# A graph network kernel: the node features and the weights are loaded from ScalarE's DMA queue, and a matrix is zeroed in rows of 5000 bytes

## The chip, the cores and the metric

The kernel runs on one core of a Trainium2 chip. The time is device time in microseconds of one execution. The program has five engines: TensorE (PE), VectorE (DVE), ScalarE (ACT), GpSimd (POOL) and SyncE (SP). SP, ACT and POOL can issue DMAs. The profile names their queues q1 (SP), q10 (ACT) and q0 (POOL). All of them move their data on the same 16 DMA engines.

## The reference

Four graph layers run one after the other on 3125 nodes with 256 features and 50,000 edges, whose destinations are sorted. Each layer normalises the features, and gathers those of the neighbours:

```
h = relu(layernorm(x));  x = x + L0(h)   # sum over edges, two products with batch norm
h = relu(layernorm(x));  x = x + L1(h)   # two weighted graph convolutions, W1, W2, Wl
h = relu(layernorm(x));  x = x + L2(h)   # one convolution, scaled by the degrees
h = relu(layernorm(x));  x = x + L3(h)   # two attention layers, 4 heads and 1
```

`_L0_gnn_ref` and `_L2_gnn_ref` use how often an edge occurs, `_L1_gnn_ref` the sum of its `edge_weight`.

## The kernel before

The kernel turns the edge list into dense matrices first. `pairs` in HBM holds for each destination and each source two numbers: the sum of the edges' weights and their count. It has 25 blocks (`NB`) of 128 destinations with 3125 sources, which is 25,000 bytes for a destination, 3.2 MB for a block and 80 MB in all. The stages that matter here are:

1. SP loads `dst`, `src`, `edge_weight` and the features `X`, then writes zeros over all 25 blocks. At most `ZQ` = 4 of these transfers are in flight: from the fifth on, SP waits for the transfer four places back, and raises `zero_ok`. Behind the last one SP issues 28 small loads (the weights and per-feature values), which all raise `w_in`.
2. DVE makes the keys of the edges (`e1`, `e2`, `key_c`), PE transposes them, ACT copies the transposed weights (`wgt`, L1000) and DVE the transposed keys (L1219). Both raise `edges_laid`, and nothing of what follows starts before both have.
3. 50 rounds (`NSC`) of 1000 edges each: PE and DVE find edges that occur twice (`same`, L1249) and sum them up (`merged`, L1271). In round 3 DVE waits for `X`, in round 30 for `w_in` (L1317).
4. POOL scatters each finished round into `pairs`, with 8 indirect DMAs that add (L555). Round t needs `merged` of t, the zeroed blocks up to `zero_ok`, and that all scatters of the round before have landed.
5. When all 50 rounds are merged, SP loads `pairs` back in 40 pieces, in rows of 5000 bytes (`pair_load`, L398). They form eight groups of 4, 4, 4, 4, 4, 2, 2 and 1 blocks with five pieces each, and a group waits until POOL's rounds that touch it are done. PE multiplies them with the features (L672) and transposes them (L692), and ACT stores the transposes (L1025, L1028) for the layers that follow.

The order of the work on each queue is the order in the code. The lines of ACT's part begin with the copy of stage 2, and there is no DMA ahead of it.

Of the kernel before, what the change touches and what calls it, by code (L numbers as in the profile page):

```python
# [16 lines left out]
Q = 125  # L17
NB = N // Q
D = 256
KT = D // 128  # L20
# [8 lines left out]
EA = 4  # L29
ECC = EC // EA  # L30
ZQ = 4
ZR = 25
KB = SC // 4
TRASH = ROWS * N
HALF = [(0, 13), (13, 12)]
# [58 lines left out]
def gnn_stack(nc, x, src, dst, edge_weight, eps0, W01, b01, g01, be01, W02, b02, g02, be02,  # L94
              W11, b11, W12, b12, Wl1, bl1, root_idx, W2, b2, W31, as31, ad31, b31, gnw, gnb, gnms,
              W32, as32, ad32, b32, out):
    with ExitStack() as ctx:
        sems = {}

        def S(name):  # L100
            if name not in sems:
                sems[name] = ctx.enter_context(nc.semaphore(name))
            return sems[name]

        def sb(name, shape, dt=F32):
            return ctx.enter_context(nc.sbuf_tensor(name, shape, dt))
# [11 lines left out]
        X = sb("X", [128, NB, D])  # L118
# [38 lines left out]
        w01, w02, w11 = [wA[:, k * KT * D:(k + 1) * KT * D].rearrange("p (k n) -> p k n", k=KT) for k in range(3)]  # L157
        w12 = wA[:, 3 * KT * D:5 * KT * D].rearrange("p (k n) -> p k n", k=2 * KT)
        wB = sb("wB", [128, 4 * KT * D])
        wl1 = wB[:, 0:2 * KT * D].rearrange("p (k n) -> p k n", k=2 * KT)  # L160
        w2, w2T = [wB[:, k * KT * D:(k + 1) * KT * D].rearrange("p (k n) -> p k n", k=KT) for k in (2, 3)]
# [7 lines left out]
        w32 = sb("w32", [128, CT, D + 2])  # L169
        va = sb("va", [128, KT, 2 * HEADS])  # L170
        cols = sb("cols", [128, 6, KT])
        colw = sb("colw", [128, 4, CT])
        bcs = sb("bcs", [128, 5, D])
        ident = sb("ident", [128, 128])
        ones = sb("ones", [128, 128])
        small = sb("small", [128, 40])
# [26 lines left out]
        idx_i = sb("idx_i", [128, 1], I32)  # L203
# [36 lines left out]
        att2 = [B[:, 2 * WIDE:2 * WIDE + D], B[:, 2 * WIDE + D:2 * WIDE + 2 * D]]  # L240
# [103 lines left out]
        colb = sb("colb", [128, 2 * KT])  # L344

        @block.sync
        def _(sp):
# [2 lines left out]
            sp.dma_start(wgt_c, edge_weight.rearrange("(c k) -> c k", k=CW)).then_inc(S("wgt_in"), 16)  # L350


            sp.dma_start(X[0:Q, :, :], x.rearrange("(j p) f -> p j f", p=Q)).then_inc(S("x_in"), 16)
            sp.wait_ge(S("zero_made"), 1)
            flat = pairs[0:TRASH, :].rearrange("(i p r c) t -> i p r (c t)", p=128, r=ZR, c=N // ZR)
            zero = R[:, 0:2 * N // ZR].unsqueeze(1).to_broadcast([128, ZR, 2 * N // ZR])
            sp.dma_start(pairs[TRASH:TRASH + SC * 128, :].rearrange("(p c) t -> p (c t)", p=128),
                         R[:, 0:2 * SC]).then_inc(S("zero_tail"), 16)
            for i in range(NB + ZQ):
# [2 lines left out]
                    sp.sem_inc(S("zero_ok"), 1)  # L362
                if i < NB:
                    sp.dma_start(flat[i], zero).then_inc(S(f"zeroed{i % ZQ}"), 16)
            w_in = S("w_in")
            nw = 0
            for t, w in ((w01, W01), (w02, W02), (w11, W11), (w12, W12), (wl1, Wl1), (w2, W2)):
                sp.dma_start(t[:, :, :], w.rearrange("(k p) n -> p k n", p=128)).then_inc(w_in, 16)
                nw += 1
            sp.dma_start(w32[:, :, 0:D], W32.rearrange("(k p) n -> p k n", p=128)).then_inc(w_in, 16)  # L370
            for k, a in enumerate((as32, ad32)):
                sp.dma_start(att2[k], a.rearrange("h c -> (h c)").partition_broadcast(128)).then_inc(w_in, 16)
            for k, v in enumerate((b11, b12, bl1, b2, b32)):
                sp.dma_start(bcs[:, k, :], v.partition_broadcast(128)).then_inc(w_in, 16)
            sp.dma_start(idx_i[:, 0:1], root_idx[0:1].partition_broadcast(128)).then_inc(w_in, 16)
            sp.dma_start(small[:, 0:1], eps0.partition_broadcast(128)).then_inc(w_in, 16)
            with nc.allow_non_contiguous_dma(reason="a few hundred per-feature values"):
                for k, v in enumerate((b01, g01, be01, b02, g02, be02)):
                    sp.dma_start(cols[:, k, :], v.rearrange("(k p) -> p k", p=128)).then_inc(w_in, 16)
                for k, v in enumerate((b12, b11)):  # L380
                    sp.dma_start(colb[:, k * KT:(k + 1) * KT], v.rearrange("(k p) -> p k", p=128)).then_inc(w_in, 16)
                for k, v in enumerate((b31, gnw, gnb, gnms)):
                    sp.dma_start(colw[:, k, :], v.rearrange("(k p) -> p k", p=128)).then_inc(w_in, 16)

            def pair_load(i):
                g, part = PUNITS[i]
                j0, nb = PG[g]
                if part == 0:  # L390
                    windows = sp.value_load(rneed[0:1, g:g + 1], min_val=1, max_val=NSC)
                    sp.wait_ge(S("rounds_done"), windows)
                    sp.sem_inc(S("pairs_begun"), 1)
                if i >= 2:
                    sp.wait_ge(S("l0_pe"), 4 * (i - 1))
                    sp.wait_ge(S("tr_pe"), PB * (i - 1))
                    sp.wait_ge(S("deg_done"), i - 1)
                sp.dma_start(PR[i % 2][:, 0:nb, :, :],  # L398
                             pair_rows[j0:j0 + nb, :, part * PW:(part + 1) * PW, :].rearrange("m p c t -> p m c t"))\
                    .then_inc(S(f"prow{i % 2}"), 16)  # L400
# [15 lines left out]
            for q in range(4 * NB):  # L416
                k, j = divmod(q, NB)
                c0, w = HALF[k % 2][0] * Q, COLS[k % 2]
# [3 lines left out]
            for q in range(4 * NB, 6 * NB):  # L422
                k, j = divmod(q, NB)
                c0, w = HALF[k % 2][0] * Q, COLS[k % 2]
                n = q - 4 * NB
# [45 lines left out]
            for q in range(STEPS * NB):  # L471
                k, j = divmod(q, NB)
# [37 lines left out]
            for q in range(STEPS * NB + LCR, (STEPS + 2) * NB):  # L510
                k, j = divmod(q, NB)
# [482 lines left out]
        @block.scalar  # L994
        def _(act):
            a = nc.scalar.activation


            act.wait_ge(S("edgeT"), 1)
# [31 lines left out]
            for i, (g, part) in enumerate(PUNITS):  # L1031
# [5 lines left out]
                for b in range(PB):  # L1037
                    n = PB * i + b
# [57 lines left out]
            for q in range(4 * NB, 6 * NB):  # L1096
                n = q - 4 * NB
                k, j = divmod(q, NB)
                w = COLS[k % 2]
# [81 lines left out]
        def _(dve):  # L1181
# [3 lines left out]

            v_.memset(R[:, 0:2 * N // ZR], 0.0).then_inc(S("zero_made"), 1)
            link.mark(v_.memset(val, 0.0))
# [645 lines left out]
```

## Time and profile before

| | |
|---|---|
| median of 3 timed runs | 4287.06 us (4277.83 to 4291.34) |
| the profiled execution | 4239.87 us |
| its span | 4238.1 us |
| busy: PE, DVE, ACT, POOL | 3434.9, 2683.2, 833.4, 650.4 us |
| moved by DMA | 523.88 MB, of it 159.74 MB written to HBM |

The span is cut into 40 slices of 106 us on the page, with a digit for the busy tenths of each engine. "Idle before, releaser" is the time in which an engine stood still ahead of an instruction, and what ended it. A queue that is called SPq or ACTq is the sequencer of that engine, which issues the DMAs; the time of such a row is how long the issue kept the engine.

### The profile page before, as it was taken

To read this page: it belongs to the slowest core of one execution; us is meant where nothing else is said; L and a number is where in the kernel's file an instruction comes from. 1 tells how busy PE (TensorE), PEld (TensorE's weight loads), DVE (VectorE), ACT (ScalarE), POOL (GpSimd) and SP (SyncE) were. 2 spreads that over 40 slices of the span, in tenths; PEclk is the share of its full clock that TensorE was granted. 3 is DMA by queue.
4 is the path that set the end of the run, shared out by engine and by line. 5 is a ranking of instruction groups with operands and counts; after the bars stand their busy time and mean duration, and the time that the engine had idled before them with its cause. 6 is when DMAs were issued, how large, how long until landed. Compare 5 with 4: busy or idle time off the path is not lost. (4 is left out here: it accounts for less than half of the span.)

```text
span 4238.1 us, 32521 instructions
## 1 busy us (share of the span) xinstructions
PE 3434.9 (81%) x12169; PEld 2015.7 (48%) x12169; DVE 2683.2 (63%) x3582; ACT 833.4 (20%) x1091; POOL 650.4 (15%) x462
## 2 busy tenths in 40 slices
PE   6830889956889999979952788888888899975898
PEld 6830867745545555444441343444344344454444
DVE  9931933312330111143449999999999999956997
ACT  0010023312420000122300222222222222232222
POOL 2555765666100000000000000000000000011000
PEclk6555589978999999989965999999999999987999
DMA  9999179967624334412135212222222223256222
GB/s 203 226 227 178 2 226 315 290 186 184 170 87 138 124 126 137 147 40 72 55 108 177 59 55 60 86 73 66 73 66 70 63 90 90 71 180 218 74 67 67
DMA packets 311726, 523.88 MB, mean 124 GB/s; under 512 B 91521, under 2 KB 232727, under 8 KB 310039
## 3 DMA queue, kind: packets, MB, share of 16 engines
q1 hardware_dynamic: 197489, 441.36, 36.1%
q0 software_dynamic: 61600, 20.44, 4.6%
q10 hardware_dynamic: 52480, 60.01, 4.4%
q8 instruction: 96, 1.57, 0.2%
q14 instruction: 61, 0.50, 0.0%
HBM read 361.99 MB, written 159.74 MB: 123 GB/s over the span
## 5 line engine op out<-in xcount | busy, mean ns | idle before, releaser
L935 PE MATMUL ps<-R,B 125*128 125x500 f32 x2800 | 1118.3, 552 | 91.7 <-DVE R L1710 87.0
L935 PEld LDWEIGHTS ps<-R,B 125*128 125x128 f32 x2800 | 513.3, 194 | 668.1 <-issue 543.0
L555 POOL DMA_INDIRECT pairs<-w x400 | 620.6, 1552 | 448.6 <-issue 257.1
L788 PE MATMUL ps<-R,H 125*128 125x500 f32 (+1 forms) x1400 | 554.0, 552 | 35.0 <-DVE R L1496 21.7
L1124 ACT ACTIVATE R<-R,asc 125x1625 f32<-125x1625 f32 (+1 forms) x200 | 320.1, 1601 | 1189.6 <-DVE R L1697 1189.5
L563 POOL DMA_DIRECT2D B<-ct_d x50 | 27.1, 546 | 2792.6 <-PE ps L935 2656.1
L1710 DVE SCALAR_TENSOR_TENSOR R<-R 125x1625 f32<-125x1625 f32 (+1 forms) x250 | 444.7, 1779 | 0.0
L788 PEld LDWEIGHTS ps<-R,H 125*128 125x128 f32 x1400 | 258.5, 195 | 316.4 <-issue 313.7
L645 PE MATMUL ps<-Fb,R 125*125 125x4 bf16 x1800 | 234.5, 248 | 202.7 <-DVE R L1249 194.7
L1697 DVE SCALAR_TENSOR_TENSOR R<-H,asc 125x1625 f32<-125x1625 f32 (+1 forms) x200 | 367.7, 1839 | 34.1 <-PE ps L935 28.0
L672 PE MATMUL ps<-R,H 125*128 125x375 f32 (+1 forms) x1000 | 305.1, 453 | 86.8 <-DMA R<-pairs 86.8
L1585 DVE SCALAR_TENSOR_TENSOR Fb<-R,asc,Fb 125x1625 f32<-125x1625 uint16 (+1 forms) x192 | 353.7, 1842 | 5.2 <-DVE ag L1610 0.2
L645 PEld LDWEIGHTS ps<-Fb,R 125*125 125x125 bf16 x1800 | 224.5, 219 | 218.6 <-issue 162.0
L935 PE MATMUL ps<-R,H 125*128 125x500 f32 (+1 forms) x700 | 276.6, 552 | 21.2 <-DVE R L1710 19.5
L1346 DVE TENSOR_TENSOR Fb<-Fb,ps 128x250 f32<-128x250 f32 (+1 forms) x140 | 67.3, 481 | 352.1 <-PE ps L672 292.6
L788 PE MATMUL ps<-R,B 125*128 125x500 f32 (+1 forms) x700 | 266.8, 538 | 1.6 <-ACT R L1081 0.9
L672 PEld LDWEIGHTS ps<-R,H 125*128 125x128 f32 x1000 | 188.1, 196 | 163.2 <-DMA R<-pairs 76.7
L1249 DVE SCALAR_TENSOR_TENSOR R<-ps,Fb,R 125x500 bf16<-125x500 f32 (+3 forms) x400 | 205.4, 536 | 2.3 <-PE ps L634 2.3
L1677 DVE TENSOR_TENSOR wB<-wB,R 125x1500 f32<-125x1500 f32 x120 | 205.6, 1713 | 0.2
L935 PEld LDWEIGHTS ps<-R,H 125*128 125x128 f32 x700 | 127.1, 194 | 164.6 <-issue 132.5
L692 PE MATMUL ps<-ident,R 125*125 125x125 f32 x1250 | 171.0, 285 | 32.0 <-ACT PT L1041 24.5
L788 PEld LDWEIGHTS ps<-R,B 125*128 125x128 f32 x700 | 126.9, 190 | 140.6 <-issue 139.4
(262 smaller groups left out, 3005.1 us busy)
## 6 DMA issues: line engine op xcount, KB each, us to landing
pairs<-R SPq DMA_DIRECT2D x25, 3125.0 KB, 38.3
R<-ct_d SPq DMA_DIRECT2D x175, 406.2 KB, 3.2
R<-ct_d SPq DMA_DIRECT2D x175, 375.0 KB, 3.1
R<-pairs SPq DMA_DIRECT2D x25, 2500.0 KB, 10.1
R<-wt_d SPq DMA_DIRECT2D x50, 812.5 KB, 4.4
R<-wt_d SPq DMA_DIRECT2D x50, 750.0 KB, 4.2
wt_d<-R ACTq DMA_DIRECT2D x13, 1250.0 KB, 7.6
wt_d<-B ACTq DMA_DIRECT2D x12, 1250.0 KB, 7.6
```

The lines of the kernel that those rows point to most:

```text
L555: pool.indirect_dma_start(pairs, bass.IndirectOffsetOnAxis(ap=key_u[:, c:c + 1], axis=0), val[:, c, :], None, compute_op=ALU.add).then_inc ...
L645: last = mm(ps[0:Q, 4 + t % 2, c * 4:(c + 1) * 4], TW[c0][:, c * Q:(c + 1) * Q], vals[:, t * SC + c0, :], start=c0 == 0 and c == 0, stop=c ...
L672: last = mm(ps[:, n % 4, 0:w], H[0:Q, j0 + m, k * 128:(k + 1) * 128], PR[i % 2][0:Q, m, o:o + w, 0], start=m == 0, stop=m == nb - 1 and no ...
L692: last = tr(ps[0:Q, 4 + 2 * (n % 2) + t, m * Q:(m + 1) * Q], PR[i % 2][0:Q, m, b * Q:(b + 1) * Q, t], ident[0:Q, 0:Q])
L788: last = mm(ps[:, bank, at:at + w], rows[0:Q, j, f * 128:(f + 1) * 128], TL[q % TS][0:Q, o:o + w], start=j == 0 and at == 0, stop=j == NB ...
L935: last = mm(ps[:, bank, at:at + w], rows[0:Q, j, f * 128:(f + 1) * 128], TT[q % TR][0:Q, o:o + w], start=j == 0 and at == 0, stop=j == NB ...
L1124: a(t, t, ACT.Exp, bias=s2).then_inc(S("l3_exp"), 1)
L1249: last = stt(TW[c][:, b * CW + lo:(b + 1) * CW], ps[0:Q, (t % 2) * 2 + b, lo:CW], k, mask, ALU.is_equal, ALU.mult, accum_out=later[0:Q, t ...
L1585: stt(dst, t, score, dst, ALU.min, ALU.max).then_inc(S(name), 1)
L1677: tt(d, d, t, ALU.add).then_inc(S("l3_den"), 1)
L1697: stt(TT[q % TR][0:Q, 0:w], u[0:Q, 0:w], s8, u[0:Q, w:2 * w], ALU.add, ALU.max).then_inc(S("l3_a"), 1)
L1710: stt(t, t, 1.0, lc, ALU.min, ALU.mult).then_inc(S("l3_t"), 1)
```

## The change

`ZR`, the number of rows into which a destination's 25,000 bytes are cut, goes from 25 to 5, so that a block is zeroed in 640 rows of 5000 bytes and not in 3200 rows of 1000. The zeros that are read come from `R[:, 0:1250]`, so DVE clears 1250 columns there and not 250. The load of `X` and the 28 loads of `w_in` leave SP's program. They stand at the start of ACT's, ahead of its first wait.

```
-ZR = 25
+ZR = 5
...
-            sp.dma_start(X[0:Q, :, :], x.rearrange("(j p) f -> p j f", p=Q)).then_inc(S("x_in"), 16)
             sp.wait_ge(S("zero_made"), 1)
             flat = pairs[0:TRASH, :].rearrange("(i p r c) t -> i p r (c t)", p=128, r=ZR, c=N // ZR)
             zero = R[:, 0:2 * N // ZR].unsqueeze(1).to_broadcast([128, ZR, 2 * N // ZR])
...
                 if i < NB:
                     sp.dma_start(flat[i], zero).then_inc(S(f"zeroed{i % ZQ}"), 16)
-            w_in = S("w_in")
-            nw = 0
-            for t, w in ((w01, W01), (w02, W02), (w11, W11), (w12, W12), (wl1, Wl1), (w2, W2)):
-                sp.dma_start(t[:, :, :], w.rearrange("(k p) n -> p k n", p=128)).then_inc(w_in, 16)
-                nw += 1
-            sp.dma_start(w32[:, :, 0:D], W32.rearrange("(k p) n -> p k n", p=128)).then_inc(w_in, 16)
...
         @block.scalar
         def _(act):
             a = nc.scalar.activation
+            act.dma_start(X[0:Q, :, :], x.rearrange("(j p) f -> p j f", p=Q)).then_inc(S("x_in"), 16)
+            w_in = S("w_in")
+            for t, w in ((w01, W01), (w02, W02), (w11, W11), (w12, W12), (wl1, Wl1), (w2, W2)):
+                act.dma_start(t[:, :, :], w.rearrange("(k p) n -> p k n", p=128)).then_inc(w_in, 16)
+            act.dma_start(w32[:, :, 0:D], W32.rearrange("(k p) n -> p k n", p=128)).then_inc(w_in, 16)
...
             act.wait_ge(S("edgeT"), 1)
```

The start of ACT's program before, where the first two rows are the table load and the copy that `edges_laid` waits for, and the third is the next table load:

```order
L1000 ACT_TABLE_LOAD
L1000 ACTIVATE Fb<-ps 125x4x100
L1008 ACT_TABLE_LOAD
L1008 ACTIVATE lns<-lns 125x25
L1011 ACTIVATE H<-X,lns 125x256 x25
```

The same place now (`wA` and `wB` hold the weights, `w` is `w32`):

```order
L974 DMA X<-in_x 125x25x256
L977 DMA wA<-in_L_gnn_W 128x2x256 x3
L977 DMA wA<-in_L_gnn_W 128x4x256
L977 DMA wB<-in_L_gnn_Wl 128x4x256
L977 DMA wB<-in_L_gnn_W 128x2x256
L978 DMA w<-in_L_gnn_W 128x8x256
L980 DMA B<-in_L_gnn_att_src 128x256
L991 DMA colw<-in_L_gnn_gn_ms 128x8x1
L995 ACT_TABLE_LOAD
L995 ACTIVATE Fb<-ps 125x4x100
```

The load of `X` and 28 more DMAs (of which some rows are left out here) now stand ahead of the copy.

The start of SP's program before, where `Fb` takes the edge list and the L357 row is a small tail of `pairs`:

```order
L348 DMA Fb<-in_dst 100x500
L349 DMA Fb<-in_src 100x500
L350 DMA Fb<-in_edge_weight 100x500
L353 DMA X<-in_x 125x25x256
L357 DMA pairs<-R 128x16
L364 DMA pairs<-R 3200x1x250 x25
L368 DMA wA<-in_L_gnn_W 128x2x256 x3
```

And now:

```order
L348 DMA Fb<-in_dst 100x500
L349 DMA Fb<-in_src 100x500
L350 DMA Fb<-in_edge_weight 100x500
L356 DMA pairs<-R 128x16
L363 DMA pairs<-R 640x1x1250 x25
L368 TENSOR_LOAD rneed
```

The zeroing moved up behind the three small loads, with 640 rows in a transfer, and the register load of the first `pair_load` follows it at once.

## Rows read from the trace of the kernel before

**Rows 1.** The page: busy tenths of the 40 slices, and the DMA engines' share.

```profile
DVE  9931933312330111143449999999999999956997
...
POOL 2555765666100000000000000000000000011000
...
DMA  9999179967624334412135212222222223256222
```

**Rows 2.** Timeline of POOL: start, duration, instruction, idle before.

```profile
65.69 1.79 POOL L555 DMA_INDIRECT pairs<-w  x1 [62.17 <-SPq L362]
...
387.75 1.55 POOL L555 DMA_INDIRECT pairs<-w  x1 [5.65 <-DMA pairs<-w]
...
426.91 1.55 POOL L555 DMA_INDIRECT pairs<-w  x1 [2.35 <-DMA pairs<-w]
...
443.64 1.55 POOL L555 DMA_INDIRECT pairs<-w  x1 [2.20 <-issue]
...
460.32 1.55 POOL L555 DMA_INDIRECT pairs<-w  x1 [2.15 <-issue]
...
1058.18 1.55 POOL L555 DMA_INDIRECT pairs<-w  x1 [4.53 <-issue]
```

**Rows 3.** Timeline of PE in the stage of the loads, and its end.

```profile
897.11 7.75 PE L672 MATMUL ps<-R,H 125*128 125x375 f32 x16 [49.73 <-DMA R<-pairs]
...
1044.26 4.92 PE L672 MATMUL ps<-R,H 125*128 125x375 f32 x8 [24.74 <-DMA R<-pairs]
...
1123.27 0.61 PE L672 MATMUL ps<-R,H 125*128 125x250 f32 x2
```

**Rows 4.** Waits up to 900 us: engine and line, waited for, us, times, longest.

```profile
DVE small L1317 <- DMA colw<-in_L_gnn_gn_ms: 157.4, 1, 157.4
...
SPq L391 <- DVE w L1271: 137.0, 1, 137.0
```

**Rows 5.** Timeline: DVE's clearing, the copy, the first duplicate search, the first merged round.

```profile
0.94 0.27 DVE L1186 MEMSET R<- 128x250 f32 x1 [0.94 <-PEq L1823]
...
18.25 0.87 ACT L1000 ACTIVATE Fb<-ps 125x400 f32<-125x400 f32 x1 [16.15 <-PE ps L623]
...
26.59 0.74 DVE L1249 SCALAR_TENSOR_TENSOR R<-ps,Fb,R 125x500 bf16<-125x500 f32 x1 [2.26 <-PE ps L634]
...
38.65 0.17 DVE L1271 TENSOR_TENSOR w<-keyf,trash 125x8 uint32<-125x8 f32 x1
```

**Rows 6.** Timeline of SP's queue: the issues, and how long each kept SP.

```profile
2.02 0.31 SPq L353 DMA_DIRECT2D X<-in_x  x1
2.37 25.06 SPq L357 DMA_DIRECT2D pairs<-R  x1
27.48 339.32 SPq L364 DMA_DIRECT2D pairs<-R  x25
388.52 1.94 SPq L368 DMA_DIRECT2D wA<-in_L_gnn_W  x4
...
409.52 0.58 SPq L383 DMA_DIRECT2D colw<-in_L_gnn_gn_ms  x1
548.10 340.79 SPq L398 DMA_DIRECT2D R<-pairs  x22
```

**Rows 7.** DMA engines' busy tenths from 0 to 60 us, 1.5 us a digit.

```profile
DMA  0463333333333333333999999999999999999999
```

**Rows 8.** Windows: stretch, busy by engine, granted clock, DMA share, GB/s.

```profile
28.50:33.00 4.50, 2.95 (x30) 2.57 (x29) 4.50 (x21) 0.00 (x0) 0.00 (x0) 0.82 1.01 335
35.00:64.00 29.00, 24.71 (x173) 23.26 (x172) 28.66 (x125) 0.00 (x0) 0.00 (x0) 0.50 1.12 238
...
554.00:558.00 4.00, 0.61 (x1) 0.50 (x2) 0.65 (x4) 0.00 (x0) 3.39 (x3) 0.50 1.11 381
```

**Rows 9.** DMA queues from 985 to 989 us: packets, MB, share.

```profile
q1 hardware_dynamic: 225, 1.05, 70.2%
...
q10 hardware_dynamic: 59, 0.05, 4.3%
```

**Rows 10.** The same from 990 to 992 us, where ACT's queue runs alone.

```profile
q10 hardware_dynamic: 614, 0.61, 92.8%
```

**Rows 11.** The same from 388 to 412 us, the 28 loads of `w_in`.

```profile
q1 hardware_dynamic: 10816, 4.09, 72.3%
```

**Rows 12.** The same from 945 to 949 us, beside scatters issued at 945.19 and 947.05.

```profile
q1 hardware_dynamic: 289, 1.45, 96.2%
```

**Rows 13.** One line of the kernel, L364: ns min, median, max of an issue.

```profile
L364 SPq DMA_DIRECT2D pairs<-R x25: 627/14252/15327, 27.5 to 352.6; - x25
```

More of the change, by code:

```diff
@@ L364, in _ @@
                     sp.dma_start(flat[i], zero).then_inc(S(f"zeroed{i % ZQ}"), 16)
-            w_in = S("w_in")
-            nw = 0
-            for t, w in ((w01, W01), (w02, W02), (w11, W11), (w12, W12), (wl1, Wl1), (w2, W2)):
-                sp.dma_start(t[:, :, :], w.rearrange("(k p) n -> p k n", p=128)).then_inc(w_in, 16)
-                nw += 1
-            sp.dma_start(w32[:, :, 0:D], W32.rearrange("(k p) n -> p k n", p=128)).then_inc(w_in, 16)
[L371 to L383, printed above, removed]
             def pair_load(i):
@@ L996, in _ @@
             a = nc.scalar.activation
+            act.dma_start(X[0:Q, :, :], x.rearrange("(j p) f -> p j f", p=Q)).then_inc(S("x_in"), 16)
[3 more added lines that the diff above has]
+            act.dma_start(w32[:, :, 0:D], W32.rearrange("(k p) n -> p k n", p=128)).then_inc(w_in, 16)
+            for k, row in enumerate((as32, ad32)):
+                act.dma_start(att2[k], row.rearrange("h c -> (h c)").partition_broadcast(128)).then_inc(w_in, 16)
+            for k, v in enumerate((b11, b12, bl1, b2, b32)):
+                act.dma_start(bcs[:, k, :], v.partition_broadcast(128)).then_inc(w_in, 16)
+            act.dma_start(idx_i[:, 0:1], root_idx[0:1].partition_broadcast(128)).then_inc(w_in, 16)
+            act.dma_start(small[:, 0:1], eps0.partition_broadcast(128)).then_inc(w_in, 16)
+            with nc.allow_non_contiguous_dma(reason="a few hundred per-feature values"):
+                for k, v in enumerate((b01, g01, be01, b02, g02, be02)):
+                    act.dma_start(cols[:, k, :], v.rearrange("(k p) -> p k", p=128)).then_inc(w_in, 16)
+                for k, v in enumerate((b12, b11)):
+                    act.dma_start(colb[:, k * KT:(k + 1) * KT], v.rearrange("(k p) -> p k", p=128)).then_inc(w_in, 16)
+                for k, v in enumerate((b31, gnw, gnb, gnms)):
+                    act.dma_start(colw[:, k, :], v.rearrange("(k p) -> p k", p=128)).then_inc(w_in, 16)
             act.wait_ge(S("edgeT"), 1)
```

## The prediction

> **What bounds the kernel now.** The page comes first, for where engines stand still. In slices 3 to 4 DVE falls to 3 and 1 tenths while the DMA engines are at 9, and POOL is busy at a middle level up to slice 10 [rows 1]. So the question is which of them sets when the first layer can start. The waits say that DVE stands 157.4 us for the last load of `w_in`, since those loads are issued behind all the zeroing; SP can therefore start loading `pairs` only at 548.10, after waiting 137.0 us for DVE [rows 4, 6]. That looks like 157 us to be won. The timelines of POOL and PE say otherwise. POOL's 50 rounds run without a pause from 65.69 to 1058.18 [rows 2], and PE waits for loaded pieces at 897.11 (49.73 us) and at 1044.26 (24.74 us), when the groups' rounds weren't done [rows 3]. The stage ends at 1123.9, 65.7 us after POOL's last round starts. **POOL's last round is the bound**; DVE's stop only eats slack, at least until POOL's end moves forward by the 50 us that PE waits at 897.
>
> POOL's rounds have three speeds, which I read from the starts of their first scatters. Beside the zeroing, 14 rounds from 65.69 to 387.75: 23.0 us each. With quiet DMA engines, 443.64 to 460.32: 16.7 us. From 426.91 to 1058.18 it is 33 rounds in 631.3 us, 80 us more than 33 x 16.7 = 551; that is what the loads and stores of the product stage cost POOL [rows 2]. A later last round follows from a start S and the zeroing's end Z: rounds at the slow speed until Z, then 16.7 each, and 80 on top.
>
> **Zeroing in 5000-byte rows.** 25 blocks of 3.2 MB are 80 MB. In rows of 1000 bytes they go at 238 GB/s, after a burst of 335 in the first 4.5 us; the loads of `pairs`, whose rows have 5000 bytes, go at 381, though they read HBM [rows 8]. So the rate lies between 238 (HBM takes no more, whatever the rows) and 381 (the engines' own pace), which is 336 to 210 us. I take 285, the middle between the sustained rate and the burst: the burst shows that short rows aren't all that limits, the drop behind it that writing may be. That is 281 us, and from a start at about 4 us Z = 285. The bounds for Z are 245 (335 GB/s; beside `X` it won't be more) and 345. Clearing 1250 columns in place of 250 is five times 0.27 us at most [rows 5], some 1 us at the start; I neglect it.
>
> **The loads on ACT's queue.** This decides. An issue is short only when the queue can take it. SP issued `X` in 0.31 us, but its next DMA, a tiny one, kept SP for 25.06 us [rows 6]: until `X` had nearly drained. The zeroing's issues of 3200 rows kept SP 14.25 us each in the median [rows 13]. I read that as: an issue is held until the one before it has been turned into rows that the engines have mostly consumed. ACT must pay the same: `X`, 28 issues behind it, and only then the copy at L995, which ran at 18.25 before [rows 5]. Behind the copy stand the key rows, the duplicate search (8.3 us later) and the first merged round (20.6 us later), and so POOL's first scatter.
>
> How long is ACT held? With nothing beside it: 25 us for `X` and 22 us for the rest (388.52 to about 410) [rows 6], so 48. But the zeroing is beside it. `X` uses only some of the engines: the digits are 3 while it runs, about 5 of 16 [rows 7], which is 3125 / 5 = 625 rows on each, 26 us / 625 = 42 ns a row. The best row on sharing is 985 to 989 us: ACT's last 1000-byte rows beside SP's 5000-byte rows come at 59 in 4 us, 15 a us, while alone ACT's queue does 614 in 2 us, 307 a us [rows 9, 10]. Some engines will have run out of ACT's rows there, so 15 is too low a bound; but it fits an engine that takes rows from its queues by turns, one long for one short, and no split by bytes. By turns, each row of `X` waits for a row of zeros of 210 ns (5000 bytes at 381/16 GB/s) to 336 ns (at 238/16): 625 x 0.25 to 0.38 = 158 to 236 us. Of the 1000 rows of zeros that each engine has (25 x 40) 375 are then left, beside 10816 / 16 = 676 packets of the 28 loads [rows 11]. So the zeroing ends first, and the remaining 300 packets go at their own pace, 300/676 of 22 us = 10 us. **ACT is free at about Z + 10 = 295 us**, 277 later than now. If the zeros and ACT's rows were generated by one unit in order of issue, ACT's 28 issues would each wait behind one of the 25 blocks, and the answer is the same.
>
> [...]
>
> **The sum.** S = 295 + 20.6 = 316, when the zeroing is over, so all rounds have the quiet speed: last round at 316 + 49 x 16.7 + 80 = 1214, against 1058. That is +156 us; what follows the last round keeps its 66 us, and all later layers their times. The stage of the loads starts at about 295 + 8 + 364 = 667 (DVE's search took 548 - 27 - 157 = 364 without its stop), when POOL is at round 21, so PE goes on waiting for POOL and the removed 157 us stop is worth nothing. The faster rounds beside no zeroing are worth 14 x 6.3 = 88 us, and are in the sum. 4240 + 156 = 4396 for the profiled execution; the timed runs' median stands 47 us above that, so 4287 + 156 = **4443 us, say 4440**. Bounds from Z: 245 gives +116, 345 gives +216; its own range is 4400 to 4505.
>
> **Rivals.** (1) ACT is held for `X` only, and the small loads slip through, or turns favour ACT's short rows: free at about 190, S = 211, three rounds beside the zeroing at 25 us: 285 + 46 x 16.7 + 80 = 1133, +75, 4360. (2) The queues share by bytes, or the short rows go ahead: ACT free at 48, S = 69, before the zeroing hurts. With (285 - 69)/23 = 9.4 rounds by Z the last starts at 285 + 39.6 x 16.7 + 80 = 1026: -32 us, **4255, faster**. With Z = 220 it is -50, 4237. For it speaks that the 15 a us may come from engines that had run out of ACT's rows; against it, that an engine with half its time for ACT's rows would have finished 59 of them in well under 4 us [rows 9, 10]. It decides at ACT free by 93 us (S = 113, last round 1059). There is a cost in it: a scatter waits behind 5000-byte rows. From 945 to 949 only SP's queue moved packets, although two scatters had been issued [rows 12]; at 30 us a round the gain shrinks to nothing (285 + 41.8 x 16.7 + 80 = 1063), which is (3), no change. (4) Zeroing at 238 GB/s or less, with the full hold: +216 or more.
>
> **Chances and range.** Full hold 0.45, more than 4505 another 0.05, held for `X` alone 0.20: slower 0.70. Rival 2 is 0.23, no change 0.07. About 0.3% (13 us) is what a measurement can tell. From 4250 to 4520 the range leaves out most of rival 2's better half and the top of rival 4.
>
> **What the profile after would show.** Right: ACTq's second row holds for well over 100 us; the ACT copy at 250 to 355; DVE and PE near 0 in slices 2 and 3; POOL's first scatter 20 us behind the copy and rounds of 16.7; zeroing over at 245 to 345; POOL's last round at about 1214; no wait at DVE's `w_in` line. Wrong: the copy before 93 us, or rounds near 30 us, or POOL's end earlier than 1058. The rate of zeroing is the weakest size, the sharing of engines the weakest step.

## The result and the profile after

| | before | after |
|---|---|---|
| timed runs, one chip | 4282.44 us (4 runs, 4273.53 to 4291.34) | 4355.07 us (4 runs, 4353.93 to 4357.18) |
| span of the profiled execution | 4238.1 us | 4354.0 us |

The ratio is 1.017, with an interval of 1.0146 to 1.0194: 73 us slower in the timed runs, 116 us in the two profiles. The forecast was 156 us slower, 4440 us in the timed runs.

The page after, with the same three rows as [rows 1]:

```profile
DVE  1079973212241111224347999999999999957897
...
POOL 0047775666500000000000000000000000001000
...
DMA  9922239968833343431125312221222223247222
```

The slices are 109 us now. DVE and POOL do next to nothing in the first two, where the DMA engines are busiest. Before, POOL was at 2 and 5 tenths there.

The timeline of ACT, with the issues on its queue. The first row is the load of `X`, the second the first of the 28 behind it, the third the last of them, and then comes the copy that all waits for:

```profile
0.82 0.57 ACTq L974 DMA_DIRECT2D X<-in_x  x1
1.42 115.88 ACTq L977 DMA_DIRECT2D wA<-in_L_gnn_W  x1
...
238.59 3.37 ACTq L991 DMA_DIRECT2D colw<-in_L_gnn_gn_ms  x1
241.99 1.28 ACT L995 ACT_TABLE_LOAD   x1 [241.99 <-issue]
243.29 0.87 ACT L995 ACTIVATE Fb<-ps 125x400 f32<-125x400 f32 x1
```

ACT is held for 242 us, and copies at 243.3 where it copied at 18.3 [rows 5]. The table load, which was made while the engine waited (at 0.82 us in the kernel before), now stands behind the issues too and adds 1.3.

The timeline of POOL:

```profile
265.68 1.79 POOL L532 DMA_INDIRECT pairs<-w  x1 [262.16 <-issue]
282.58 1.55 POOL L532 DMA_INDIRECT pairs<-w  x1 [2.15 <-DMA pairs<-w]
299.38 1.55 POOL L532 DMA_INDIRECT pairs<-w  x1 [2.26 <-DMA pairs<-w]
...
1167.39 1.55 POOL L532 DMA_INDIRECT pairs<-w  x1 [5.70 <-issue]
```

The first scatter is 200 us later than before, the rounds then have the quiet speed of 16.7 to 16.9 us up to the stage of the loads, and the last round starts 109 us later (1167.4 against 1058.2, [rows 2]). The faster rounds gave 91 of the 200 us back. PE still waits for POOL's rounds:

```profile
1000.29 7.49 PE L649 MATMUL ps<-R,H 125*128 125x375 f32 x16 [66.52 <-DMA R<-pairs]
...
1152.40 5.37 PE L649 MATMUL ps<-R,H 125*128 125x375 f32 x8 [26.06 <-DMA R<-pairs]
```

These answer to [rows 3], where it was 49.73 and 24.74 us. The 157.4 us for which DVE stood for `w_in` [rows 4] are gone from the waits, and they brought nothing.

The windows of the zeroing (8 to 110 and 110 to 220 us), columns as in [rows 8], and the DMA digits from 220 to 246 us, 0.65 us a digit:

```profile
8.00:110.00 102.00, 2.49 (x10) 1.87 (x10) 9.70 (x17) 0.00 (x0) 0.00 (x0) 1.00 0.99 394
110.00:220.00 110.00, 0.00 (x0) 0.00 (x0) 0.00 (x0) 0.00 (x0) 0.00 (x0) 1.00 1.01 377
```

```profile
DMA  9999999999565333333333333333348221080000
```

The DMA engines move 394 and 377 GB/s in all. The zeros' share of it, on SP's queue, is 371 and 335 (37.87 and 36.83 MB); from 4 to 227 us it is 78.75 MB, or 353 GB/s, above the 335 that I took as the upper bound. At 227 us the digit falls to 3 (SP's queue takes 30.8% of the 16 engines from 229 to 238 us, about 5), and stays there until about 240. I take these for the five that carried `X` and so have zeros still to write; the profile doesn't name them, but with `X` cut over all engines (`after_xsplit`, below) there is no such stretch: the digits fall from 9 to 0 between 222 and 226 us. ACT is free when they are done.

### The profile page after: what moved, and what is told of

It reads as the page before. It is cut to its first block and busy times, and to the rows that moved or that the text cites. A ratio compares the mean times of both kernels' runs of the same rounds, so it can differ in the third digit from the quotient of the medians.

```text
span 4354.0 us, 32521 instructions
## 1 busy us (share of the span) xinstructions
PE 3449.3 (79%) x12169; PEld 2023.6 (46%) x12169; DVE 2684.8 (62%) x3582; ACT 833.4 (19%) x1091; POOL 650.2 (15%) x462
## 5 line engine op out<-in xcount | busy, mean ns | idle before, releaser
L912 PEld LDWEIGHTS ps<-R,B 125*128 125x128 f32 x2800 | 515.9, 195 | 671.5 <-issue 546.8
L611 PE MATMUL ps<-ident,Fb 125*125 125x125 f32 x400 | 100.8, 433 | 230.2 <-DVE Fb L1230 230.2
```

Source lines behind the costliest of these rows:

```text
L912: last = mm(ps[:, bank, at:at + w], rows[0:Q, j, f * 128:(f + 1) * 128], TT[q % TR][0:Q, o:o + w], start=j == 0 and at == 0, stop=j == NB ...
```

## The experiments

All were timed against the kernel before on their own chip. There the kernel before took 4242 to 4243 us, not 4282. "Last round" is the start of POOL's last round of scatters.

**The kernel before again.** No edit.

> The kernel before, unchanged, so that a second profile of it stands beside timed runs of the same chip. Its profiled execution was 4240 us, its timed runs 4274 to 4291. If the gap is a matter of the chip or the day (theory chip), profile and timed runs of this one agree within 5 us, and their common time shows whether 4240 or 4285 is the rule. If the profiled execution is always shorter than the timed ones (theory profiling), the gap of 40 us comes again. In the trace I look at the rounds of POOL beside the zeroing (23.0 us each before) and at the start of its last round (1058 before).

Measured: 4244.0 us in 10 runs, its profile's span 4245.5, the kernel before 4242.7 in 18 runs; ratio 0.9998 (0.9986 to 1.001). Profile and timed runs agree. So a profiled execution isn't shorter by nature, and 4282 us is particular to the first comparison (its chip or its hour; which of them isn't shown). The last round starts at 1058.77.

**Only the rows.** From the kernel before:

```
-ZR = 25
+ZR = 5
```

> Only ZR = 5; all loads stay on SP, so ACT copies at 18 us. Zeroing from 27 us at 400 GB/s, over at about 230, the loads of w_in done by 255 and no stop of DVE. Theory queue depth: a scatter waits behind a number of rows, so five times as long rows make POOL's rounds beside the zeroing 30 us or more; 5.5 of them, last round at 1037, time 20 us under before. Theory bytes in flight: rounds stay at 23 us, 7 of them, last round at 1008, 50 us under before. If the zeroing in short rows had cost nothing, the time would be that of before.

Measured: 4179.5 us, ratio 0.9843 (0.9818 to 0.9867), 63 us faster. The timeline of POOL:

```profile
42.01 1.79 POOL L555 DMA_INDIRECT pairs<-w  x1 [38.49 <-SPq L362]
64.93 1.55 POOL L555 DMA_INDIRECT pairs<-w  x1 [8.16 <-DMA pairs<-w]
...
227.63 1.55 POOL L555 DMA_INDIRECT pairs<-w  x1 [7.69 <-DMA pairs<-w]
...
996.80 1.55 POOL L555 DMA_INDIRECT pairs<-w  x1 [4.51 <-issue]
```

Eight rounds from 42.01 to 227.63 are 23.2 us each, where 1000-byte rows had 23.0: rows five times as long don't make the scatters beside them slower. POOL also starts 24 us sooner (42.01 against 65.69), as the first block is zeroed sooner; I had not counted that. The last round is at 996.8, where "bytes in flight" had 1008 and "queue depth" 1037.

**The loads on ACT's queue beside short rows.** From the changed kernel:

```
-ZR = 5
+ZR = 25
```

> The change with ZR = 25: loads on ACT's queue, rows of 1000 bytes. Theory turns (each DMA engine takes one row of each queue in turn): a row of X waits for a row of 60 to 70 ns and not of 200, so X takes 65 to 75 us in place of 127, the rest about as long, ACT copies at 130 to 150 us; POOL starts at 150 to 170, 8 to 9 rounds of 23 us beside the zeroing that lasts to 345 to 360, last round at 1100 to 1115, 40 to 60 us over before. Theory bytes (the queues share by bytes): X takes 52 us with any row length, the copy is at 80 to 100, with 5000-byte rows as with these, and the last round comes by 1075.

Measured: 4269.1 us, ratio 1.0066 (1.0045 to 1.0087), 26 us slower. The timeline of ACT:

```profile
1.42 53.34 ACTq L977 DMA_DIRECT2D wA<-in_L_gnn_W  x1
...
108.84 0.87 ACT L995 ACTIVATE Fb<-ps 125x400 f32<-125x400 f32 x1
```

The issue behind `X` holds ACT for 53 us and not for 116, so the length of the other queue's rows matters; but the hold, the copy (109) and the last round (1085.5) were all sooner than "turns" had them, and 53 is also what sharing by bytes gives here. This run alone is not clear between them; the next is.

**And beside rows of 25000 bytes.** The same with

```
-ZR = 5
+ZR = 1
```

> The change with ZR = 1: zeroing in rows of 25000 bytes, 200 on each DMA engine. Theory turns, one row of each queue: the 625 rows of X on its five engines outlast the 200 rows of zeros, so X is done only after the zeroing (215 to 230 us), the issue behind X holds ACT for 220 to 240 us in place of 116, the rest goes alone in 22, ACT copies at 245 to 270, last round at 1170 to 1195, time 5 to 25 us over the changed kernel's. Theory bytes: the hold behind X stays at about 116 us, and the time at the changed kernel's or under it.

Measured: 4335.0 us, ratio 1.0222 (1.0205 to 1.0239), the same as the changed kernel's on that chip. The timeline of ACT, and the queues from 60 to 120 us (packets, MB, share), first for this kernel and then for the changed one:

```profile
1.42 210.71 ACTq L977 DMA_DIRECT2D wA<-in_L_gnn_W  x1
...
238.57 0.87 ACT L995 ACTIVATE Fb<-ps 125x400 f32<-125x400 f32 x1
```

```profile
q1 hardware_dynamic: 1142, 25.48, 99.0%
q10 hardware_dynamic: 345, 0.35, 1.7%
```

```profile
q1 hardware_dynamic: 4377, 21.38, 88.3%
q10 hardware_dynamic: 1302, 1.33, 6.3%
```

SP's packets lie on 16 engines (99.0%), those of `X` on 5: from 5 to 27 us of the kernel before, `X` runs alone at a share of 33.4%, and cut over all engines, from 5 to 12 us of `x_split`, at 104.9% (its packets overlap), so 33.4% is 16 x 33.4/104.9 = 5.1 engines. So an engine took 1142/16 = 71 packets of SP and 345/5 = 69 of `X` here (64 of the 71 are rows of zeros, 25.48 MB in all; the others have under 512 bytes), and 274 and 260 in the changed kernel: **one for one, with rows of 25,000 bytes as with 5000**. By bytes that is about 25 to 1 and 5 to 1. Do the engines turn after every row, or after a group? From 62 to 63 us:

```profile
q1 hardware_dynamic: 17, 0.40, 93.1%
q10 hardware_dynamic: 5, 0.01, 1.4%
```

In each of the five us from 61 to 66 ACT's queue moves 5 packets, one for each engine of `X`, and a row of zeros takes 0.94 us there (64 on an engine in 60 us). So an engine turns after a single row.

The hold of 211 us settles it against bytes. The copy came at 239 and not at 245 to 270, since the rest behind `X` took 25 us with the zeroing over, and the zeroing was over sooner.

**The changed kernel again**, on that chip.

> The changed kernel once more, on the chips of the experiments, where the kernel before takes 4243 us in 18 timed runs and not 4282. If the chip matters for both kernels, this one takes about 4315, 1.7% over before again. If it matters only for what the kernel before waits for (POOL's scatters beside the zeroing), this one stays at 4355, and the ratio is 1.026.

Measured: 4335.5 us, ratio 1.0221 (1.0204 to 1.0238), 92 us slower; the copy at 239.9, the last round at 1154.9. So both kernels took longer in the first comparison, before by 39 us and after by 20; neither guess had that.

**The copy first.** From the changed kernel, the copy moved ahead of the 29 DMAs:

```
+            act.wait_ge(S("edgeT"), 1)
+            a(wgt.rearrange("p (c i) -> p i c", i=EA), ps[0:Q, 5, 0:EC].rearrange("p (i c) -> p i c", i=EA), ACT.Copy)\
+                .then_inc(S("edges_laid"), 1)
+
             act.dma_start(X[0:Q, :, :], x.rearrange("(j p) f -> p j f", p=Q)).then_inc(S("x_in"), 16)
...
-            act.wait_ge(S("edgeT"), 1)
-            a(wgt.rearrange("p (c i) -> p i c", i=EA), ps[0:Q, 5, 0:EC].rearrange("p (i c) -> p i c", i=EA), ACT.Copy)\
-                .then_inc(S("edges_laid"), 1)
```

> The change with all 29 DMAs of ACT behind its copy of the edges' weights. If ACT's hold is what made the change slower, the copy is at 18 us, POOL starts at 40 to 50, DVE stops in round 3 for X until about 150 us, and w_in has landed by 245, before round 30; POOL's rounds from 155 on, 3 to 4 of them slow, last round at about 1030 to 1040, and the time is 20 to 30 us under before. If the loads beside the zeroing cost time in another way than by holding ACT, it stays near the changed kernel's 4355.

Measured: 4228.5 us, ratio 0.9964 (0.9953 to 0.9975), 14 us faster, not quite the 20 to 30 expected. The copy is at 19.29; the issue behind `X` now holds ACT for 133 us, from 19.9 to 153, but nothing that POOL's first rounds need stands behind it. What is late next is `X` for DVE, in its timeline:

```profile
171.65 0.43 DVE L1268 BATCH_NORM_STATS2 st<-X 125x6 f32<-125x256 f32 x1 [114.75 <-DMA X<-in_x]
```

POOL does three rounds from 42.30, stands for 73 us until 179.81, and begins the last at 1044.9. The hold ahead of the copy is what made the change slower: moving it is worth 107 us (4335.5 to 4228.5, on two chips whose kernels before agree within 1 us).

**X alone on ACT.** From the changed kernel; the 28 others are back on SP, behind the zeroing:

```
             act.dma_start(X[0:Q, :, :], x.rearrange("(j p) f -> p j f", p=Q)).then_inc(S("x_in"), 16)
-            w_in = S("w_in")
-            for t, w in ((w01, W01), (w02, W02), (w11, W11), (w12, W12), (wl1, Wl1), (w2, W2)):
...
```

> 5000-byte rows, X issued by ACT as in the change, the 28 other loads back on SP behind the zeroing. Theory hold (an issue is held until the one before it has nearly drained; X itself holds nobody): ACT copies at 19 us, POOL starts at 42. X lands at about 120, so DVE stands some 70 us in round 3, which costs POOL about 10; the last round starts at 1000 to 1015, the time is 45 to 60 us under before. If a large load held the queue's own engine, the copy would be at 115 us or later.

Measured: 4200.4 us, ratio 0.9901 (0.9884 to 0.9917), 43 us faster. ACT copies at 19.29 though `X` is issued ahead of the copy, at 0.82 and in 0.56 us. In the changed kernel the issue behind it took 115.88: the load holds the next issue, not its engine. DVE stands 81.8 us for `X` and POOL's last round is at 1017.4, two us past my range, as the time is.

**X over more engines.** From the changed kernel:

```
-            act.dma_start(X[0:Q, :, :], x.rearrange("(j p) f -> p j f", p=Q)).then_inc(S("x_in"), 16)
+            xv = x.rearrange("(j p) f -> p j f", p=Q)
+            act.dma_start(X[0:112, :, :], xv[0:112, :, :]).then_inc(S("x_in"), 16)
+            act.dma_start(X[112:Q, :, :], xv[112:Q, :, :]).then_inc(S("x_in"), 16)
...
-                    dve.wait_ge(S("x_in"), 16)
+                    dve.wait_ge(S("x_in"), 32)
```

> The change with the load of X cut into partitions 0 to 111 and 112 to 124, which use 16 and 13 DMA engines where the whole uses 5. Theory turns, engine by engine: 200 rows of X on an engine and not 625, so the hold behind X is 40 to 50 us and not 116; 676 more turns with zeros beside them bring ACT's copy to 180 to 200, no engine lags at the end of the zeroing, last round at 1095 to 1115, 50 to 65 us under the changed kernel. Theory bytes: the hold behind X goes by bytes, the same 3.2 MB against the same zeros, and shrinks only to 80 or so.

Measured: 4264.3 us, ratio 1.0055 (1.0038 to 1.0071), 71 us under the changed kernel on the same chip. The timeline of ACT:

```profile
1.25 7.33 ACTq L976 DMA_DIRECT2D X<-in_x  x1
8.61 14.94 ACTq L979 DMA_DIRECT2D wA<-in_L_gnn_W  x1
...
155.41 0.87 ACT L997 ACTIVATE Fb<-ps 125x400 f32<-125x400 f32 x1
```

The hold behind `X` is 22 us for both parts, less than the 40 to 50 of "turns", and far from the 80 of "bytes"; the copy is at 155 and the last round at 1080. Is a turn cheaper than a full row of zeros, then? ACT's loads lie on all engines here. For `X` the trace of `x_split` shows it, where SP's queue runs alone: a share of 104.9% from 5 to 12 us for the first part, and from 15.2 to 16.2 us 190 rows of `X` beside 15 rows of zeros. A row of zeros takes 0.19 us (2485 in 30 us on 16 engines, below), so 15 in 1 us are 3 engines, and the other 13 still carry the second part. The rows of the weights have a share of 95.1% alone (`act_rows1`, 212.13 to 216 us); for the 4-byte rows I take it from the equal numbers below. So the packets of the two queues can be compared as they are: from 40 to 80 us, where most of ACT's rows have 1024 bytes, and from 120 to 150, where they have some 4 bytes.

```profile
q1 hardware_dynamic: 2828, 13.82, 83.5%
q10 hardware_dynamic: 2827, 2.78, 19.7%
```

```profile
q1 hardware_dynamic: 2485, 12.14, 98.8%
q10 hardware_dynamic: 2484, 0.01, 4.7%
```

It is not: one packet goes for one, even 4 bytes for 5000. What makes the holds shorter than "turns" had them is their end and their start. The issue behind `X` is let go while rows of `X` are still to move: at 23.5 us, when the hold ends, ACT's queue has moved 2230 packets of 3125, so some 56 rows on each of 16 engines are left. In the changed kernel it is 2759 of 3125 at 117.3, 73 on each of five; in `act_rows25` 2667 at 54.76, so 92; in `act_rows1` 2569 at 212.13, so 111. And 1127 of the packets went in the first 9 us, when few zeros stood beside them.

**Two blocks in flight.** From `rows5_only`, `ZQ = 2` in place of 4.

> 5000-byte rows with all loads on SP, as in rows5_only (4179 us, 63 under before), but with 2 blocks of zeros in flight and not 4. POOL's rounds beside the zeroing took 23.2 us there and 16.7 without. If the 6.5 us come from all rows that are queued (theory backlog), half as many in flight halves them: eight rounds shorter by 3 us each, 20 to 25 us off the time. If they come from what the DMA engines have already taken up (theory taken up), the rounds stay at 23 us, the zeroing loses a little rate at most, and the time is 4175 to 4190.

Measured: 4176.2 us, ratio 0.9844 (0.9829 to 0.9859), the same as with four. Nine rounds from 42.49 to 245.88 are 22.6 us each, against 23.2 with four in flight, where "backlog" had 3 us less: the rounds hardly feel what is queued behind.

**All loads on SP, X over more engines.** From `rows5_only`, `X` cut as above.

> rows5_only with the load of X, still first on SP, cut into partitions 0 to 111 and 112 to 124. X then takes 9 to 12 us in place of 26, so the zeroing starts at 10 to 13 and ends some 15 us sooner. POOL's first scatter can't come before the first merged round at 40 us, where it is 42 now, so only the end of the zeroing gains: 15 us fewer at 23 in place of 16.7 us a round, 4 to 6 us off the time, 4170 to 4178. A theory by which the wait for X or its bandwidth still matters to POOL would have 15 us or more.

Measured: 4165.0 us, ratio 0.9821 (0.9805 to 0.9836), the fastest of all: 77 us under before and 14 under `rows5_only`, a comparison across two chips whose kernels before agree within 1 us. The timelines of SP and of POOL's last round:

```profile
2.40 8.34 SPq L355 DMA_DIRECT2D X<-in_x  x1
10.78 1.23 SPq L359 DMA_DIRECT2D pairs<-R  x1
12.06 193.30 SPq L366 DMA_DIRECT2D pairs<-R  x25
```

```profile
979.94 1.55 POOL L557 DMA_INDIRECT pairs<-w  x1 [4.26 <-issue]
```

The zeroing begins 15 us sooner and the last round 17 us sooner, where I expected 4 to 6. Its rounds beside the zeroing take 22.4 and not 23.2 us; after ten rounds POOL is 7 us ahead (260.02 against 267.50), and the rest of the 17 us arose later, in rounds beside the loads. Why those were shorter is open.

## Why the prediction was right and wrong

**What bounds the kernel** was read rightly: POOL's last round. The page's idle time pointed at DVE's 157 us stop. It is gone after, and the kernel is slower. In every profile here the kernel ends 3177 to 3187 us after POOL's last round begins.

**The hold of ACT** was right in kind. ACT was free only when the zeroing was, and copying first or leaving the 28 loads on SP took the loss away. The issue behind `X` is let go when 56 (`after_xsplit`) to 111 rows (`act_rows1`) are left on an engine, which I had put as "mostly consumed". **The turns** were right as well, one row for one row. That I read this from 59 packets beside 225 [rows 9] was thin; the 2828 to 2827 packets are the evidence, and the 5 packets of `X` in each us, one an engine, show that no group of rows is taken before the turn. The other reading in the prediction, one unit that works in order of issue, does not hold: in the changed kernel six issues of ACT pass between 165.98 and 177.50 us, while SP issues a block of zeros every 8.6 us (25 in 215.25).

**The step that failed is the term of the zeroing.** "I take 285, the middle between the sustained rate and the burst" and, in the bounds, "335 GB/s; beside X it won't be more". Measured: 353 GB/s of zeros up to 227 us, beside `X` and the 28 loads, and 385 with these. So the zeroing was through at about 227 us, with a tail on five engines to about 240, and not at 285; even the tail is under my bound of 245. All that hangs on it moves along: ACT free at 242 and not 295, first scatter at 265.7 and not 316, last round at 1167.4 and not 1214. The same size is wrong in the 158 to 236 us for the rows of `X`: from 20 to 60 us ACT's queue moves 875 packets, 175 on each of five engines, which is 229 ns a turn and not 250 to 380; ACT was past `X` at 117.3. With 265.7 put into the sum of the prediction, it gives 265.7 + 818 + 80 = 1164, 3 us off. Its own bound of 245 gave +116, and the profiles are 116 apart. That is partly luck: the last rounds are 109 apart, and the other 7 us came behind them, where I had expected nothing; two profiles of the kernel before differ there by as much (3179.9 and 3186.7 us). The loads' 381 GB/s in rows of the same length [rows 8] was the nearest row for 5000-byte rows, and I left it because they read HBM and the zeroing writes it. Writing was not the limit of the 238 GB/s, with 353 written here; the short rows were.

**A second error is in the base.** Of the 83 us by which the loss was overstated (156 against 73), the profiles hold 40 (156 against 116). The other 43 are the distance between the first profile of before (4240) and the timed runs beside it (4282). I had added it to both kernels, "4287 + 156". It didn't apply to the changed kernel, whose profile (4355.7) and timed runs (4355.1) agree. In the experiments the two kernels are 92 us apart (4243 and 4335.5), with the last rounds 96 us apart in `after_again` and `before_again`. What slowed the kernel before more than the changed one in the first comparison isn't settled: no profile of before exists whose time is that of those timed runs.

**Rival 2** (faster, ACT free at 48) did not occur. Its cost, scatters behind long rows at 30 us a round, was a misreading: [rows 12] show 4 us without a packet of a scatter beside a load, but the rounds beside 5000-byte zeros are 23.2 us as beside 1000-byte ones. So the rows alone were the gain, 63 us, and the move of the loads turned it into a loss. The forecast summed both and never priced the first by itself. Rival 1 (ACT held for X only) didn't occur either: after X the 28 loads took 125 us more, against 22 alone.

## What to carry to other kernels

In these runs the DMA issue behind a large transfer held the engine that issued it until that transfer had nearly drained: 25 us behind `X` alone. Beside a busy neighbour queue every row of the transfer waited for one row of the neighbour, measured with 5000 and with 25,000 bytes. So the hold grew with the neighbour's row length (53, 116 and 211 us beside rows of 1000, 5000 and 25,000 bytes) and with the transfer's rows on its fullest engine (116 us with 625 rows in the changed kernel, 22 with 200 in `after_xsplit`). So nothing an engine must do early belongs behind such an issue: do the early work first, or issue from the queue that has nothing else to do. When an edit has two parts, price each alone: here one was worth -1.6% and the other turned it into +2%.

## What the runs showed of the hardware

- Zeros were written to HBM in rows of 1000 bytes at 238 GB/s (before, 35 to 64 us) and at 225 beside scatters (64 to 350 us); in rows of 5000 at 390 beside scatters (`rows5_only`, 40 to 200 us) and at 400 beside 4-byte rows (`after_xsplit`, 110 to 200 us); in rows of 25000 at 424 beside the rows of `X` (`act_rows1`, 20 to 110 us).
- Two queues on one DMA engine went packet for packet: 2828 to 2827 with rows of 5000 bytes against mostly 1024 (`after_xsplit`, 40 to 80 us), 2485 to 2484 with 5000 against 4 (120 to 150 us), about 71 to 69 on an engine with 25000 against 1024 (`act_rows1`, 60 to 120 us).
- The issue behind the 3125 rows of `X` was let go before these were through: 73 rows an engine were left in the changed kernel, 56 in `after_xsplit`, 92 in `act_rows25`, 111 in `act_rows1`.
- POOL's rounds beside the zeroing took 23.0 us on average at 1000 bytes a row (before, 65.69 to 387.75 us) and 23.2 at 5000 (`rows5_only`, 42.01 to 227.63), and 22.6 with two blocks in flight in place of four (`zq2`, 42.49 to 245.88), against 16.7 alone (before, 443.64 to 460.32).
- `X`, a load of 125 partitions, ran on about 5 engines (33.4% of the 16 from 5 to 27 us of before, 26 us alone). Cut into 112 and 13 partitions, on 16 and then 13 engines, the same bytes held SP's next two issues for 8.3 and 1.2 us in place of 25 (`x_split`).
